# A four-layer graph network on one core: heads of its stages rearranged

## What is computed

```python
# layer 0
A_norm = relu((A + A.T) * 0.5);  D = sum(A_norm, axis=1)
L_norm = eye(N) - D**-0.5[:, None] * A_norm * D**-0.5[None, :]
out = relu(einsum('nm,bmo->bno', L_norm, einsum('bnf,fo->bno', H, W)))
# layer 2, after two convolutions h = relu(adj @ (h @ Wg + bg)), each
for p in range(1, 5):                       # windows of p nodes
    wins = h[:, :nw * p].reshape(B * nw, p, Hd)
    h[:, arange(nw) * p + p - 1] = lstm_last(Wih[p-1], Whh[p-1], bih[p-1], bhh[p-1], wins)
# layer 3
A_hat = (A + eye(n)) * dinv[:, None] * dinv[None, :]
agg = einsum('nm,bmd->bnd', A_hat, features)      # then linear, batch norm, relu, linear, batch norm
```

## Time and profile before

| what | value |
|---|---|
| median of 3 runs | 3039.32 us (3038.06 to 3040.39) |
| profiled execution | 3033.48 us |
| its span, first to last instruction | 3031.7 us |
| TensorE matmul busy | 2749.6 us (91%) |
| VectorE busy | 1659.9 us (55%) |
| ScalarE busy | 1323.7 us (44%) |
| GpSimd busy | 171.7 us (6%) |
| mean granted TensorE clock | 0.968 |

### The profile page before, as it was taken

How to read it: one execution, slowest core, us unless ns; L and a number is a source line. 1 busy time by engine, 2 the same in 40 slices (tenths; PEclk the granted TensorE clock), 3 DMA queues, 4 the chain that set the end, 5 groups by cost and what they waited for, 6 DMA issues and landing times. The chain is left out here.

```text
span 3031.7 us, 38525 instructions
## 1 busy us (share of the span) xinstructions
PE 2749.6 (91%) x14565; PEld 2319.6 (77%) x14565; DVE 1659.9 (55%) x3195; ACT 1323.7 (44%) x2150; POOL 171.7 (6%) x98
## 2 busy tenths in 40 slices
PE   6799998899999969999999996998989868999987
PEld 6678887899999958888877875777777757778743
DVE  8766765577777643213322124888787863331246
ACT  2665454566666532112211113666767663221235
POOL 2000102000001000000000000001010000000000
PEclk9999997999999979999999998999999989999999
DMA  8544543322223153223322113011212135231258
GB/s 347 175 152 164 179 163 142 101 69 85 70 70 98 43 179 110 66 64 136 111 73 65 55 66 139 15 42 28 84 28 56 28 83 193 94 95 48 87 197 304
DMA packets 240837, 326.18 MB, mean 108 GB/s; under 512 B 13680, under 2 KB 155024, under 8 KB 235920
## 3 DMA queue, kind: packets, MB, share of 16 engines
q1 hardware_dynamic: 237200, 311.25, 31.7%
q10 hardware_dynamic: 3456, 12.58, 1.0%
HBM read 227.17 MB, written 96.62 MB: 107 GB/s over the span
## 5 line engine op out<-in xcount | busy, mean ns | idle before, releaser
L986 PE MATMUL l_acc<-l_a_hi,l_g_hi 128*128 128x512 f32 x1536 | 602.3, 392 | 38.0 <-DVE l_g_lo L917 28.7
L986 PE MATMUL l_acc<-l_a_lo,l_g_hi 128*128 128x512 f32 x1536 | 599.2, 390 | 0.0
L986 PE MATMUL l_acc<-l_a_hi,l_g_lo 128*128 128x512 f32 x1536 | 598.8, 390 | 0.0
L909 DVE TENSOR_TENSOR l_a_lo<-l_raw,l_a_hi 128x512 fp32r<-128x512 f32 x192 | 132.8, 691 | 752.9 <-ACT l_a_hi L859 752.9
L1442 PE MATMUL n_acc<-n_hb,n_p 128*128 128x129 f32 x4096 | 472.6, 276 | 24.7 <-DVE n_p L1358 19.5
L859 ACT ACTIVATE l_a_hi<-l_raw 128x512 fp32r<-128x512 f32 x192 | 121.1, 631 | 845.6 <-PE l_acc L986 818.8
L1442 PEld LDWEIGHTS n_acc<-n_hb,n_p 128*128 128x128 f32 x4096 | 464.5, 192 | 28.8 <-issue 15.1
L986 PEld LDWEIGHTS l_acc<-l_a_hi,l_g_hi 128*128 128x128 f32 x1536 | 289.3, 188 | 99.8 <-DVE l_g_lo L917 28.9
L1358 DVE SCALAR_TENSOR_TENSOR n_p<-n_e,n_cols,c_mT 128x2048 f32<-128x2048 f32 x128 | 296.8, 2346 | 89.3 <-ACT n_e L1319 71.0
L2053 ACT ACTIVATE r_gate<-r_ps,r_bias 128x512 f32<-128x512 f32 (+2 forms) x504 | 297.1, 639 | 110.6 <-PE r_ps L2214 77.4
L986 PEld LDWEIGHTS l_acc<-l_a_lo,l_g_hi 128*128 128x128 f32 x1536 | 289.3, 188 | 61.1 <-issue 1.4
(11 more groups left out here) (261 smaller groups left out, 3782.7 us busy)
## 6 DMA issues: line engine op xcount, KB each, us to landing
l_raw<-in_adjT_dram SPq DMA_DIRECT2D x256, 256.0 KB, 2.8
l_raw<-in_rows_dram SPq DMA_DIRECT2D x64, 256.0 KB, 3.0
l_hraw<-h SPq DMA_DIRECT2D x32, 512.0 KB, 3.4
z<-l_res SPq DMA_DIRECT2D x64, 256.0 KB, 2.7
m_z<-z SPq DMA_DIRECT2D x16, 1024.0 KB, 5.0
l_xt<-in_x_dram SPq DMA_DIRECT2D x30, 512.0 KB, 3.4
d_xt<-in_x_dram SPq DMA_DIRECT2D x16, 512.0 KB, 18.2
n_hb<-h SPq DMA_DIRECT2D x8, 1024.0 KB, 5.8
```

The costliest lines, as they stand in the source:

```text
L909: dve.tensor_tensor(a_lo[:, gp % RING], raw[:, gp % RING], a_hi[:, gp % RING].bitcast(F32), ALU.subtract).then_inc(a_low, 1)
L986: last = pe.matmul(acc[:, b], lhs[:, s, b * D:(b + 1) * D], rhs[:, gp % RING], start=(s == 0 and lhs is g_hi and rhs is a_hi), stop=(s == ...
```

## The change

Four edits at the heads of stages. In `degrees` the order of loads (and of VectorE's work with it) has one x tile after each row tile in place of two, and the reduction of the diagonals (L299) moves behind the steps that form the degrees, with the counts of `own` moved accordingly. In `laplacian` ScalarE's second `total` moves behind the first `high`, and VectorE's second `add` behind the first `low`. In `spread` VectorE makes `fix(1)` and `fix(2)` after the first `low` and the first features. In `recurrences` the first block goes: SP loads the first level of `wih`, then hT of the first pair in eight blocks of 512 columns, the biases, and the other weights behind them, staged in `xt`; ScalarE and VectorE split the first level and the eight blocks one by one, and six further weight blocks (levels 1 to 3 of both tensors) at the start of units 1, 2 and 3 of pair 0. TensorE waits block by block, and for the weights of a level before its first unit. SP loads x only when the last weight block is split, since `xt` holds the weights till then.

```diff
--- before.py
+++ after.py
@@ -195,7 +195,7 @@
 
     order = [("x", 0), ("x", 1), ("x", 2)]
     for t in range(T):
-        order += [("a", t)] + [("x", k) for k in (2 * t + 3, 2 * t + 4) if k < T]
+        order += [("a", t), ("x", t + 3)] if t + 3 < T else [("a", t)]
     with ExitStack() as ctx:
         up = prog.sb(ctx, "d_up", [P, UPPER[T]])
         lo = prog.sb(ctx, "d_lo", [P, UPPER[T]])
@@ -254,7 +254,7 @@
                 pool.wait_ge(measured, g + 1)
                 pool.tensor_tensor(scale[:, g * GW:(g + 1) * GW], var[:, g * GW:(g + 1) * GW],
                                    half[:, g * GW:(g + 1) * GW], ALU.pow).then_inc(powered, 1)
-            pool.wait_ge(own, 4)
+            pool.wait_ge(own, 3)
             pool.tensor_tensor(keep["dinv"][:, :], small[:, 1], keep["halves"][:, :], ALU.pow).then_inc(powered, 1)
 
         @block.scalar
@@ -296,17 +296,17 @@
                     at = slice(g * GW, (g + 1) * GW)
                     dve.tensor_scalar(mean[:, at], mv[:, at, 0], -1.0, None, ALU.mult)
                     dve.tensor_scalar(var[:, at], mv[:, at, 1], EPS, None, ALU.add).then_inc(measured, 1)
-            dve.tensor_reduce(keep["dia"][:, :], diag[:, :, :], AX.X, ALU.add).then_inc(own, 1)
             dve.wait_ge(relued, T)
             dve.wait_ge(columned, 1)
             total, safe, flag = small[:, 0], small[:, 1], small[:, 2]
             dve.tensor_scalar(total[:, 0:1], sym[:, 0:1], 1.0, None, ALU.mult)
             dve.tensor_tensor(total[:, 1:T], sym[:, 1:T], pc[:, 1:T], ALU.add).then_inc(own, 1)
+            dve.wait_ge(own, 1)
+            dve.tensor_scalar(flag, total, 0.0, None, ALU.is_equal).then_inc(own, 1)
             dve.wait_ge(own, 2)
-            dve.tensor_scalar(flag, total, 0.0, None, ALU.is_equal).then_inc(own, 1)
+            dve.scalar_tensor_tensor(safe, total, 0.5, flag, ALU.mult, ALU.add).then_inc(own, 1)
             dve.wait_ge(own, 3)
-            dve.scalar_tensor_tensor(safe, total, 0.5, flag, ALU.mult, ALU.add).then_inc(own, 1)
-            dve.wait_ge(own, 4)
+            dve.tensor_reduce(keep["dia"][:, :], diag[:, :, :], AX.X, ALU.add).then_inc(own, 1)
             dve.tensor_scalar(keep["ndeg2"][:, :], safe, -2.0, None, ALU.mult)
             dve.wait_ge(powered, GROUPS)
             dve.tensor_tensor(mean[:, :], mean[:, :], scale[:, :], ALU.mult).then_inc(own, 1)
@@ -506,11 +506,12 @@
                 act.dma_start(io["h1"][t], normal(t)).then_inc(h_out, 16)
 
             total(0)
-            total(1)
             for gp in range(PIECES):
                 if gp < T:
                     features(gp)
                 high(gp)
+                if gp == 0:
+                    total(1)
                 total(gp + 2)
                 if gp >= T and gp % T == FINISH:
                     finish(gp // T - 1)
@@ -631,8 +632,11 @@
             for gp in range(PIECES):
                 if gp < T:
                     features(gp)
-                add(gp + 1)
+                if gp:
+                    add(gp + 1)
                 low(gp)
+                if gp == 0:
+                    add(1)
                 if gp >= T and gp % T == FINISH:
                     finish(gp // T - 1)
                 if gp >= T and gp % T in ADD:
@@ -958,12 +962,15 @@
                         continue
 
             fix(0)
-            fix(1)
             for gp in range(TOTAL):
-                fix(gp + 2)
+                if gp:
+                    fix(gp + 2)
                 low(gp)
                 for h in h_after(gp):
                     features(h)
+                if gp == 0:
+                    fix(1)
+                    fix(2)
                 if ended_at(gp) is not None:
                     finish(ended_at(gp))
             finish(len(chunks) - 1)
@@ -1890,7 +1897,15 @@
         LAST_HALF = T // 2
         last_own, last_done = prog.sem("r_last_own"), prog.sem("r_last_done")
         sem, sems = (lambda s: prog.sem(f"r_{s}")), (lambda s: prog.sems(f"r_{s}"))
-        w_in, b_in, w_high, w_split = sem("w_in"), sem("b_in"), sem("w_high"), sem("w_split")
+        w_in, b_in, w_high, w_split = prog.sems("r_w_in", 3), sem("b_in"), sem("w_high"), sem("w_split")
+        first_in = [prog.sems(f"r_first_in{k}", SKIP) for k in pair]
+        first_high, first_split = sems("first_high"), sems("first_split")
+        parts = ("wih", "whh")
+        level = lambda l: slice(l * G4, (l + 1) * G4)
+        staged = [xt[k][:, :, :].rearrange("p t f -> p (t f)") for k in pair]
+
+        BEHIND = {n: [(k, n + 1) for k in range(2)] for n in range(SKIP - 1)}
+        block_of = lambda s: slice(RESIDUE_AT[s] * 512, RESIDUE_AT[s] * 512 + 512)
         b_ready = sem("b_ready")
         h_in, raw_high, raw_split = sems("h_in"), sems("raw_high"), sems("raw_split")
         summed, activated = sems("summed"), sems("activated")
@@ -1900,42 +1915,6 @@
         turned, x_done, h_done, h_out, last_out = (sem(s) for s in (
             "turned", "x_done", "h_done", "h_out", "last_out"))
         batch_view = lambda d: d.rearrange("t p b f -> b p t f")
-        with ExitStack() as c1:
-
-
-            block = c1.enter_context(nc.Block())
-
-            @block.sync
-            def _(sp):
-                for k, name in enumerate(("wih", "whh")):
-                    sp.dma_start(hx[k][:, :].rearrange("p (l g) -> p l g", g=G4), weights[name]).then_inc(w_in, 16)
-                for k, name in enumerate(("bih", "bhh")):
-                    sp.dma_start(bias[:, k], weights[name]).then_inc(b_in, 16)
-                for k in pair:
-                    sp.dma_start(raw[k][:, :], io["hT"][k]).then_inc(h_in[k], 16)
-
-            @block.scalar
-            def _(act):
-                act.wait_ge(w_in, 32)
-                for k in range(2):
-                    act.activation(w_hi[:, k].rearrange("p l g -> p (l g)"), hx[k][:, :], ACT.Copy).then_inc(w_high, 1)
-                for k in pair:
-                    act.wait_ge(h_in[k], 16)
-                    act.activation(raw_hi[k][:, :], raw[k][:, :], ACT.Copy).then_inc(raw_high[k], 1)
-
-            @block.vector
-            def _(dve):
-                dve.wait_ge(b_in, 32)
-                dve.tensor_tensor(bias[:, 2], bias[:, 0], bias[:, 1], ALU.add).then_inc(b_ready, 1)
-                for k in range(2):
-                    dve.wait_ge(w_high, k + 1)
-                    dve.tensor_tensor(w_lo[:, k].rearrange("p l g -> p (l g)"), hx[k][:, :],
-                                      w_hi[:, k].rearrange("p l g -> p (l g)").bitcast(F32),
-                                      ALU.subtract).then_inc(w_split, 1)
-                for k in pair:
-                    dve.wait_ge(raw_high[k], 1)
-                    dve.tensor_tensor(raw_lo[k][:, :], raw[k][:, :], raw_hi[k][:, :].bitcast(F32),
-                                      ALU.subtract).then_inc(raw_split[k], 1)
         block = ctx.enter_context(nc.Block())
         NPAIR = B // 2
         NRAW = sum(u.p == 1 for u in units)
@@ -2001,9 +1980,20 @@
                         sp.wait_ge(x_out[k], i * 16 + 16)
                         load_x(i + 1, k)
 
+            sp.dma_start(staged[0][:, level(0)], weights["wih"][:, 0]).then_inc(w_in[0], 16)
+            for s in range(SKIP):
+                for k in pair:
+                    sp.dma_start(raw[k][:, block_of(s)], io["hT"][k][:, block_of(s)]).then_inc(first_in[k][s], 16)
+                if s == 1:
+                    for k, name in enumerate(("bih", "bhh")):
+                        sp.dma_start(bias[:, k], weights[name]).then_inc(b_in, 16)
+            for k, name in enumerate(parts):
+                sp.dma_start(staged[k][:, G4:].rearrange("p (l g) -> p l g", g=G4), weights[name][:, 1:])\
+                  .then_inc(w_in[1 + k], 16)
+            next_h(0)
+            sp.wait_ge(w_split, 2 * SKIP - 1)
             for k in pair:
                 load_x(0, k)
-            next_h(0)
             with sp.Fori(1, NPAIR - 1) as i:
                 next_h(i)
                 store(i - 1, True)
@@ -2041,6 +2031,21 @@
 
         @block.scalar
         def _(act):
+            def first_parts():
+                act.wait_ge(w_in[0], 16)
+                act.activation(w_hi[:, 0, 0], staged[0][:, level(0)], ACT.Copy).then_inc(w_high, 1)
+                for s in range(SKIP):
+                    for k in pair:
+                        act.wait_ge(first_in[k][s], 16)
+                        act.activation(raw_hi[k][:, block_of(s)], raw[k][:, block_of(s)], ACT.Copy)\
+                           .then_inc(raw_high[k] if s == SKIP - 1 else first_high[k], 1)
+                act.wait_ge(b_ready, 1)
+
+            def split_weights(n):
+                for k, l in BEHIND[n]:
+                    act.wait_ge(w_in[1 + k], 16)
+                    act.activation(w_hi[:, k, l], staged[k][:, level(l)], ACT.Copy).then_inc(w_high, 1)
+
             def evaluate(i, n, k, late):
                 size = units[n].size
```

(35 more changed lines are left out.)

## The result

The changed kernel takes **3025.36 us** (median of 6 runs, 3016.05 to 3029.06) where the kernel before, on the same chip, takes 3038.69 (6 runs, 3036.40 to 3040.39): ratio 0.9958, 95% interval 0.9947 to 0.9970. The forecast was 3027.0, faster. Two repeats gave 3025.89 (0.9956, 0.9942 to 0.9969) and 3023.72 (0.9953, 0.9940 to 0.9966). The gain by the medians of the three is 13.3, 13.6 and 15.6 us. The profiled execution of after took 3023.62, span 3021.83.

A forecast was written before the change was run, and what follows sets the result against it. TensorE is busy for 91% of the span, so time is won only where it stands still or runs slower. 1.2 + 2.0 + 6.3 + 2.8 = 12.3 us gives 3021.2 profiled, plus the 5.84 offset 3027.0; range 3020 to 3034.

The forecast's parts named there:

- Part 1: Degree stage: respaced loads free TensorE's late block; VectorE and GpSimd then end it; 1.2 us won, range -1 to 2.5.
- the late end: Degree stage: VectorE behind, reaching x15 at 69.1 at the latest; of 0.9 to 2.5 us won, 1.2 taken.
- Part 2: Laplacian head: second total and addition put off, first matmul 4.5 us earlier, of which 2.0 counts; range 0 to 4.4.
- the ring: Laplacian's first chunk: three pieces in rotation, paced from the second piece, shrink the 4.5 us earlier start to 2.1.
- (a): Only the LSTM edit and some of layer three's count; Laplacian returns its 2.0, degrees gain nothing: 3030 to 3035; chance 0.2.
- Part 3: LSTM head: first gate 11.1 to 9.4 us earlier, less 4.0 to 4.1 for six splits; 6.3 won, range 3 to 8.
- Part 4: Layer three's head: low half needs the first piece alone, 3.3 us earlier; 2.8 won, range 1.5 to 3.4.
- the loss to the lower clock: Layer three's start: TensorE's clock may rise up to 2 us later after the new start, costing 1.0 us.
- (b): LSTM units 1 to 3: TensorE falls to its lower clock, the split weights win only 1.9; 3031.4 us; chance 0.1.
- (c): More than forecast: VectorE keeps up in degrees, blocks land at full rate, Laplacian keeps its early start; 3022.4; chance 0.12.
- (d): LSTM head: small loads land one by one, first gate 12.5 us later, 16.5 lost there; 3049.8; chance 0.03.
- (e): LSTM's early start waits at the hand-over to pair 1, degree and Laplacian gains fade; 3 to 5 won, 3035; chance 0.05.

## Why the prediction held, point by point

**Part 1** (1.2 forecast, 1.4 measured). The step held: TensorE's block dissolves, and x15's statistics, aggregation and the two powers end the stage. The take-up of x15 was put at 67.5 to 69.1 and the late end chosen; it was 68.05, so the step was sized on the safe side. That x15's statistics and GpSimd behind them are what is late was shown by moving x15 (1.76 earlier gave 1.8). The hidden reduction cost nothing in either place. One reading was a little off: a step's matmuls are not less than its bytes at every t, by its own formulas they are 6.45 against 6.39 us at t = 0; nothing hung on it.

**Part 2** (2.0 forecast, 1.5 measured as a mean, 1.9 in the first profile). First matmul 4.2 earlier (4.5 forecast), second piece 1.8 in the first profile and 2.1 in the mean of all (2.1 forecast). That the chunk follows the second piece and not the first matmul agrees with this, since no execution won more than 2.7 of the 4.2; no run moved the second piece alone, so it isn't shown further. That the ring keeps the 2.1 was too firm. In the first profile TensorE has six waits of 0.35 to 0.97 us within the chunk, and between executions the chunk's end moves by 3 us. Rival (a) had said that the ring could give it back; it does so in two of nine.

**Part 3** (6.3 forecast, 8.2 measured) was right in sign and mis-sized in three terms. The gain of the first gate was over-estimated: 8.6 us, over eight executions 8.1 to 9.2, where 9.4 to 11.1 were given, because the last block is in only 11.0 us after the first load (10.5 to 11.5 in the eight), not 8.5 to 10.1: 414 GB/s without a pause was too fast. The splits cost 3.36, not 4.0 to 4.1: in the rows VectorE's operations last 0.69 but start 0.60 apart, so six are 3.6, and the price per operation should have been taken from start to start. Left is 5.3. The third term was not in the sum: TensorE's clock later in the stage. The second stream's sixteen transposes at the end of pair 0, in stretches for these tiles alone (TensorE, weight loads, VectorE, in the first view ScalarE too, then granted clock, DMA share and GB/s), in the kernel before:

```profile
2019.40:2022.70 3.30, 3.12 (x16) 2.75 (x16) 0.00 (x0) 0.00 (x0) 0.60 0.00 0
```

and in the kernel after:

```profile
2012.30:2014.40 2.10, 1.94 (x16) 1.73 (x16) 0.00 (x0) 1.00 0.00 0
```

Behind the same pause of 1.93 us they take 3.12 us at a granted clock of 0.60, or 1.94 at 1.00. That is the 1.2 between 5.3 and the 6.5 of the first profile. All four executions of the LSTM before have these slow transposes and a unit 5 of 9.9 us; each of the six after is spared one of the two: the transposes take 1.94, or unit 5 takes 8.4. Pairs 1 to 3, from there to the last LSTM matmul, are 1.1 shorter in the mean as well (456.0 and 454.9), but two of the four before have 454.8 and 455.1, so this much of the 8.2 is scatter between executions. Nor is the spared stretch a gain that the change guarantees: the kernel with the biases moved, whose gate comes 1.8 later, is spared neither, with a unit 5 of 9.95 and transposes of 3.05, which is most of the rest of its 621.86. So what the edit itself is shown to be worth is the 5.3 at its head; whether the remainder comes again with another start of the stage is open.

**Part 4** (2.8 forecast, 3.3 measured). The 3.3 of an earlier start were right; the loss to the lower clock that I took off did not come (405.30 against 405.22 from first to last matmul).

**The sum** (12.3 forecast, 14.4 by stages, 13.3 to 15.6 by the medians) is low mainly by what part 3 gained behind its head. That it comes so near is in part luck: part 3's head gave 1.0 less than forecast, and 2.9 came from later stretches that no term of the sum had. Of the rivals, (a) fell with parts 1, 2 and 4 in the sum, though its ring does take part 2 back at times. (b) fell: in units 1 to 3 of the first profile TensorE keeps its full clock (granted 1.00, matmuls of 0.39), and VectorE is the bound. (c) was not reached: the blocks paused and the ring kept no more than 2.7. (d) fell: the loads overlap, the eleven are in after 11.0 us and not 32. (e) fell: the gains of parts 1 and 2 are in the sum, and the LSTM stage is 8.2 shorter. The offset of 5.84 from the profiled execution to the median was 1.74 for after (3023.62 and 3025.36): single executions scatter by more, and what was tested is the difference.

## What to carry to other kernels

Where two engines take turns, an added operation was free only inside the pause of the one that does it: four subtractions cost 2.4 us at the heads of busy units, most of it again at the heads of later ones, and nothing one by one in gaps of 0.6 to 0.8 us. Price an engine that is the bound by the distance from start to start, not by the length of its rows. And small loads at a head gave back in overlap what they lost in pauses, so weigh the last landing plus what is left to do behind it, not the landing alone.
